# Half-position scans of a two-layer vision kernel: VectorE's weighing of a state moved behind the next state's scan

## What is computed

```python
def step(h, inp):
    dtt, ut, bt, ct = inp
    dA = jnp.exp(dtt[..., None] * A)
    h = h * dA + (dtt * ut)[..., None] * bt[:, :, None, :]
    y = jnp.einsum('bkdn,bkn->bkd', h, ct)
    return (h, y)
...
h = jax.nn.gelu(jnp.einsum('bsd,edh->ebsh', x, w1) + b1[:, None, None, :], approximate=False)
y = jnp.einsum('ebsh,ehd->ebsd', h, w2) + b2[:, None, None, :]
```

## Time and profile before

| what | us |
|---|---|
| median of 3 runs (lowest, highest) | 5605.96 (5604.6, 5613.72) |
| the profiled execution | 5607.85 |
| its span, first to last instruction | 5606.0 |
| a convolution stage, first scan to end of last (24 lanes) | 720.8 |
| a Mamba stage, the same (12 lanes) | 363.4 |
| all six stages together | about 3250 |

### The profile page before, as it was taken

How to read it: one execution, slowest core, us unless ns; L and a number is a source line. 1 busy time by engine, 2 the same in 40 slices (tenths; PEclk the granted TensorE clock), 3 DMA queues, 4 the chain that set the end, 5 groups by cost and what they waited for, 6 DMA issues and landing times. The chain is left out here.

```text
span 5606.0 us, 73119 instructions
## 1 busy us (share of the span) xinstructions
PE 4828.6 (86%) x23205; PEld 3411.3 (61%) x23205; DVE 4445.6 (79%) x4529; ACT 3634.0 (65%) x5725; POOL 3960.4 (71%) x3074
## 2 busy tenths in 40 slices
PE   7888797789898887888989888888998988888998
PEld 5776546656666645555666645565666654556777
DVE  6889838959999848977999957996999975896544
ACT  5666455448887757767878857775878865775222
POOL 5888619839999818857999935894999962984111
PEclk9999999989999998998999999998999999999999
DMA  5777607737877616647788724654877842562110
GB/s 206 263 252 264 211 10 258 252 132 254 287 268 268 226 34 219 224 135 250 260 280 271 269 69 171 220 183 161 281 266 276 271 166 102 201 216 93 43 43 29
DMA packets 356676, 1104.83 MB, mean 197 GB/s; under 512 B 33210, under 2 KB 121126, under 8 KB 354872
## 3 DMA queue, kind: packets, MB, share of 16 engines
q1 hardware_dynamic: 356280, 1100.06, 56.9%
HBM read 1086.24 MB, written 13.68 MB: 196 GB/s over the span
## 5 line engine op out<-in xcount | busy, mean ns | idle before, releaser
L1157 PE MATMUL banks<-ident,prod 128*128 128x128 f32 x4752 | 764.9, 287 | 392.5 <-DVE prod L1458 286.6
L1157 PEld LDWEIGHTS banks<-ident,prod 128*128 128x128 f32 x4752 | 556.8, 145 | 799.1 <-DVE prod L1458 557.8
L1449 DVE TENSOR_TENSOR_SCAN banks<-banks,h 128x512 f32<-128x512 f32 x594 | 723.3, 1218 | 85.8 <-ACT banks L1297 48.5
L1400 POOL TENSOR_TENSOR h<-lane,Bb 128x512 f32<-128x512 f32 x576 | 722.8, 1272 | 57.8 <-DMA Bb<-half_rows 33.8
L1297 ACT ACTIVATE banks<-lane,A 128x512 f32<-128x512 f32 x864 | 581.1, 686 | 251.6 <-DVE prod L1458 82.4
L1229 PE MATMUL banks<-w_a,Cb 128*128 128x384 f32 x1536 | 552.2, 488 | 0.0
L1449 DVE TENSOR_TENSOR_SCAN banks<-banks,half_carry_a,h 128x512 f32<-128x512 f32 x396 | 505.5, 1277 | 8.8 <-ACT banks L1297 4.9
L1400 POOL TENSOR_TENSOR h<-half_du_a,Bb 128x512 f32<-128x512 f32 x384 | 482.7, 1275 | 14.8 <-DMA Bb<-half_rows 10.1
L1297 ACT ACTIVATE banks<-half_delta_a,A 128x512 f32<-128x512 f32 x576 | 385.3, 685 | 151.5 <-DVE lane L1430 73.7
L1217 PE MATMUL banks<-big,w_a 128*128 128x256 f32 x1728 | 435.0, 394 | 1.0 <-DMA w_a<-w_in 0.8
L1458 DVE TENSOR_TENSOR prod<-banks,half_C_a 128x512 f32<-128x512 f32 x528 | 365.3, 692 | 73.4 <-DMA half_C_a<-half_rows 2.4
(11 more groups left out here) (471 smaller groups left out, 12291.6 us busy)
## 6 DMA issues: line engine op xcount, KB each, us to landing
Bb<-half_rows SPq DMA_DIRECT2D x576, 512.0 KB, 4.3
C_first<-rows SPq DMA_DIRECT2D x288, 512.0 KB, 5.4
Cb<-half_rows SPq DMA_DIRECT2D x288, 512.0 KB, 4.4
w_a<-w_in SPq DMA_DIRECT2D x256, 576.0 KB, 6.1
w_b<-w_in SPq DMA_DIRECT2D x128, 576.0 KB, 6.2
half_C_a<-half_rows SPq DMA_DIRECT2D x128, 512.0 KB, 6.7
Bb<-rows SPq DMA_DIRECT2D x96, 512.0 KB, 5.5
half_C_b<-half_rows SPq DMA_DIRECT2D x64, 512.0 KB, 6.6
```

Of the source, the lines that this page charges most:

```text
L1157: mm = eng.matmul(ps[:, 0, at], src[:, at], m.ident[:, :], start=n == 0 and k == 0, stop=added(s) == (i + 1) * N, is_transpose=True, skip_ ...
L1400: eng.tensor_tensor(m.dBu[:, s % DRIVES, :], m.du[i % 2], m.B[b % BRING][:, cols(s % 2)], ALU.mult).then_inc(st.dbu, 1)
L1449: eng.tensor_tensor_scan(flip(to), flip(slot(s)), flip(m.dBu[:, s % DRIVES, :]), initial, ALU.mult, ALU.add).then_inc(st.scanned, 1)
```

## The change

VectorE's `weigh(s - 1)` now stands behind `scan(s)`, no longer behind its own scan. TensorE's `add` of a state that VectorE weighs moves one step later as well, and with it the last `back`; `lane_order`, from which the counts of finished additions are taken, follows. Three products of TensorE go one step later too (`dt_product` from step 0 to 1, the gate products and the out products from step 6 to 7), since the banks that they take are freed by a `weigh` that is now later. What ScalarE, GpSimd and SyncE issue, and in which order, is the same as before.

```diff
--- before.py
+++ after.py
@@ -852,10 +852,10 @@
     COPY_AT, BACK_AT, TAKE_AT, SUM_AT, DELTA_AT = 3, 4, 7, 8, 4
     SKIP_TAKE_AT = 9
     BEHIND = 2
-    GATE_AT, PRODUCT_AT, OUT_AT, OUT_COPY_AT = 9, 6, 9, 11
+    GATE_AT, PRODUCT_AT, OUT_AT, OUT_COPY_AT = 9, 7, 9, 11
     gated = range(1, TILES + 1) if products is not None else ()
     product_of = {TILES + 2 + f: f for f in range(CT)} if products is not None else {}
-    INPUT_AT, INPUT_PLACE_AT, INPUT_TAKE_AT = 6, 9, 11
+    INPUT_AT, INPUT_PLACE_AT, INPUT_TAKE_AT = 7, 9, 11
     input_lanes = sorted(inputs.at) if inputs is not None else []
     input_of = {i: k for k, i in enumerate(input_lanes)}
     input_done = {inputs.at[i]: k + 1 for k, i in enumerate(input_lanes)} if inputs is not None else {}
@@ -883,7 +883,7 @@
 
         return s - pooled(s)
 
-    lane_order = [a for b in range(N) for a in ([] if by_pool(b) else [b]) +
+    lane_order = [a for b in range(N + 1) for a in ([b - 1] if b and not by_pool(b - 1) else []) +
                   ([b - BEHIND] if b >= BEHIND and by_pool(b - BEHIND) else [])]
 
     def added(s):
@@ -935,7 +935,7 @@
     downs = {pair_at(v, 2) + k: 2 * v + k for v in range(PAIRS_IN) for k in range(2)}
 
     evicts = {pair_at(v, 2) + 3: (v + 1) * 2 // PER - 1 for v in range(PAIRS_IN) if (v + 1) * 2 % PER == 0}
-    LAST = max([STEPS] + [s + 7 for s in evicts])
+    LAST = max([STEPS + 1] + [s + 7 for s in evicts])
 
     def chunk(k):
         return guests[k // E][0]
@@ -1235,9 +1235,9 @@
 
                 if s in ups and n == 0:
                     up(ups[s])
+                if s and s <= STEPS and not by_pool(s - 1):
+                    add(s - 1)
                 if s < STEPS:
-                    if not by_pool(s):
-                        add(s)
                     if n >= BEHIND and by_pool(s - BEHIND):
                         add(s - BEHIND)
                     if i and n == BACK_AT:
@@ -1248,11 +1248,11 @@
                         gate_product(input_of[i])
                     if fresh(i + 2) and n in (PROJECT_AT - 3, PROJECT_AT - 2):
                         project(i + 2, n - PROJECT_AT + 3)
-                    if i + 1 < LANES and n == DELTA_AT - 4:
+                    if i + 1 < LANES and n == DELTA_AT - 3:
                         dt_product(i + 1)
                     if i in turned_of and n == TURN_AT:
                         turn_residual(turned_of[i])
-                if s == STEPS - 1:
+                if s == STEPS:
                     back(LANES - 1)
                 if s in ups and n:
                     up(ups[s])
@@ -1489,15 +1489,16 @@
                 i, n = s // N, s % N
                 if s < STEPS:
                     scan(s)
-                    if not by_pool(s):
-                        weigh(s)
+                if s and s <= STEPS and not by_pool(s - 1):
+                    weigh(s - 1)
+                if s < STEPS:
                     if n == TAKE_AT and i:
                         take(i - 1)
                     if i in gated and n == GATE_AT:
                         gate(i - 1)
                     if i + 1 < LANES and n == DELTA_AT + 1:
                         delta(i + 1)
-                if s == STEPS - 1:
+                if s == STEPS:
                     take(LANES - 1)
                 if s in evicts:
                     evict(evicts[s])
```

## The result

The changed kernel takes 5653.8 us (median of 4 runs, 5644.7 to 5659.1) where the kernel before takes 5605.6 in the same job: a ratio of 1.0078, 95% interval 1.0061 to 1.0096. It is slower, by some 44 us. The forecast of 5616 was 38 us too low, and its likeliest band, 5594.8 to 5617.2 (0.43), was missed: slower had 0.38. The time lies inside the range, close to its upper end, and next to the rival on TensorE's clock (5659, chance 0.15).

The account below looks back on a forecast made before the run. VectorE was taken to bound the kernel; its 257 us saved would become stall on ScalarE's banks. 3 x 1.5 + 3 x 2.5, less about 2, gave + 10 on 5606: 5616 us, range 5570 to 5662.

Parts of the forecast that it names:

- the rival on TensorE's clock: TensorE idles some 3 us at every lane's turn, its clock falls, late up products delay a Gelu: 43 us, 5659; chance 0.15.
- What the change saves: VectorE's scan and weighing no longer wait for each other: 0.22 us off each of 1188 steps, 257 us of VectorE's time.
- The rival that the 0.13 us stay: VectorE's gap between scan and weighing stays even with a scan between, every link grows by 0.22: 5725; chance 0.03.
- The sentence quoted from the Trainium skill's page: "The semaphore costs nothing extra here": an operation flushes the pipeline anyway, so the 257 us would be nothing; the forecast disagreed.
- The ring takes it back: Banks are freed a scan later, ScalarE's lead shrinks from three scans to two, VectorE's saving is stall at states 3, 9, 14.
- the walk: Lane time followed link by link between scans 3, 6, 9, 14 and next 3; convolution averages 30.35 and 29.25 us; chance 0.62.
- The sum for the ring: Three convolution stages at + 1.5 and three Mamba stages at + 2.5, less about 2 for hidden stalls: + 10 us.
- the link that was to decide: The clock costs time once the second up product ends behind the first table load's start; 0.4 of 0.7 us margin left.
- a sign that the walk is wrong: Stalls released by GpSimd or TensorE instead of ScalarE's decays, or lanes of 28 us and less.
- The three products of TensorE that move are ready before their readers by more than a step: TensorE's products moved one step later were forecast to make no reader wait.
- GpSimd at nothing: GpSimd needs 27.6 us of a lane, 1 to 2 less than forecast lanes; cost nothing, up to 10 us if cover goes.
- The Mamba stages: Input lanes go from 31.44 to 32.5 us, other first-half lanes within 0.3, second-half lanes lose 0.2: + 2.5 a stage.

Follow-up runs that it names:

- run 4: Changed kernel with the experts' Gelu computed as Identity and the table loads left out (output not the reference's): 5502.7 us, ratio 0.9825.
- run 5: Kernel before with Gelu computed as Identity and the table loads left out (output not the reference's): 5557.8 us, ratio 0.9902.
- run 7: Run 6 plus the delta's product back at step 0 and state 0 weighed and added in its own step: 5596.8 us, ratio 0.9979.
- run 6: Changed kernel plus ten filler matmuls on TensorE at the lane's turn, in the convolution stages alone: 5613.5 us, ratio 1.0015.
- run 1: Changed kernel plus ten filler matmuls on TensorE at the lane's turn, in all stages: 5631.8 us, ratio 1.0046.
- run 2: Kernel before plus six filler matmuls on TensorE in its idle time at the lane's turn: 5602.0 us, ratio 0.9995.
- run 11: Changed kernel without fillers, state 0 weighed and added in its own step, delta's product back at step 0: 5643.5 us, ratio 1.0080.
- run 3: Changed kernel with VectorE weighing states 5, 9 and 14 in their own step, TensorE's order unchanged: 5632.7 us, ratio 1.0052.
- run 8: Run 7 with states 0, 5, 9 and 14 weighed and added in their own step in all stages: 5594.8 us, ratio 0.9970.
- run 10: Run 7 with early states 0, 5, 9, 14 (convolution) and 0, 6 (Mamba), plus four drive buffers instead of three: 5563.0 us, ratio 0.9919.

## Why the prediction was right or wrong

- **What the change saves: right.** 0.21 us between a dependent and an independent pair were forecast from the rows, and the pairs came out so. The rival that the 0.13 us stay is refuted. The sentence quoted from the Trainium skill's page "VectorE: DVE Perf Modes", section "The DRAIN you can't avoid", is said there of a chain of eight copies, and does not hold for this pair. The rows differ by 0.21 us (scan ends to weighing, + 0.13 behind its own scan and - 0.08 at 1428.44 above).
- **The ring takes it back: right, and shown.** Each piece of the walk is within 0.07 us of its undisturbed lanes, and with the blocks cut the change gains 43 us on the old order by the ratios (runs 4 and 5).
- **The sum for the ring: 22 us too high.** With both other costs mended (run 7) the kernel is 0.21% faster than before, 12 us, where the walk gave + 10 (run 7 also weighs state 0 early, which was not walked). The lanes are not what is off: behind the first three of the first stage they take 30.39 and 29.06 us in run 7, and 30.46 and 29.26 in run 6, where the walk has 30.35 and 29.25. Part of it is the base. The forecast took 29.75 us for a first-half lane before the change; the mean over the lanes after the first three is 29.97 (5.64, 6.62, 8.32, 9.39) and 29.76 for the second instead of 29.7, so each convolution stage was forecast 3.3 us too dear: it was to get 1.5 us longer and takes 718.4 us in run 7 against 721.3. Another 3.7 us a stage lie behind the last scan, a stretch that wasn't walked (157.4 us before, 153.7 in run 7).
- **TensorE's clock: the cost that was given as a rival, 0.15.** Its size was nearly right (43 us forecast, some 35 measured), but by luck: it was 0.4 us for a waiting Gelu in each of 108 lanes, and what came is some 13 us in each of the three convolution stages, for other readers. The measured time lies in the range because this size had been taken in. Right was how it starts: the copy of the sum is later, the idle time doubles, the clock falls. What was wrong is the link that was to decide. I made it whether the second up product ends behind the start of the first table load. It does: it ends at 1733.47 + 1.94 = 1735.41, and the load starts at 1734.32, 1.1 us earlier, where the forecast left a margin of 0.4. But the load waits for nothing, the Gelu behind it starts at 1735.62, and the whole convolution stage has one wait of 1.7 us there. ScalarE's timeline in that lane:

```profile
1733.61 0.69 ACT L1297 ACTIVATE banks<-lane,A 128x512 f32<-128x512 f32 x1 [1.09 <-DVE prod L1458]
1734.32 1.28 ACT L1341 ACT_TABLE_LOAD   x1
1735.62 0.84 ACT L1341 ACTIVATE Cb<-banks,vec 128x256 f32<-128x256 f32 x2
```

  Who waits is VectorE, for the turned sum and the down products that stand behind the ups in TensorE's queue. Its waits of the first convolution stage (us, times, longest):

```profile
DVE xt_a L1485 <- PE banks L1229: 13.0, 9, 1.6
DVE big L2946 <- PE banks L1201: 4.8, 4, 2.1
```

  The pieces show the same. With the fillers (run 6) those from 6 to 9, where the turned sum is taken and the eviction stands, add up to 10.3 us less in the first stage (176.2 to 165.9), and those from 3 to 6, where ScalarE waits for the delta's product, to 5.2 less (139.6 to 134.4). Stalls released by TensorE were named as a sign that the walk is wrong; here they came beside it.

  I had followed the first reader of the late product and not the queue behind it. With that reader alone the chance of 0.15 looked fair; with the queue it should have been the likeliest case, as the lane of the earlier trace rows already showed the low level before the change. Runs 1 and 6 agree with the warning of gaps in the Trainium skill's page "TensorE: Matmul & The Clock Gate", section "Why this matters for your kernels", though the gaps here (1.16 and 2.48 us) are shorter than the one that it names. Run 2 adds a limit: what low clock the kernel before has costs it nothing.
- **"The three products of TensorE that move are ready before their readers by more than a step": wrong for one of them.** The delta's activations waited for theirs in 9 of the first stage's lanes, up to 1.0 us each, and behind them the piece from 3 to 6 grew to 6.1 to 6.5. Run 7 puts 17 to 20 us on it, together with the early weighing of state 0, once the clock is mended; run 11 finds nothing to 10 us while it is not.
- **GpSimd at nothing: right for this change,** with 11.2 us of wait in the stage against 9.7. It was the next in line as soon as the ring was loosened (runs 3, 8 and 10).
- **The Mamba stages: + 7.5 forecast, + 14.6 measured over the three, and + 4.1 in run 7.** From state 6 on the input lanes came as walked. Part of the surplus is the delta's product: 3 to 6 is up to 0.8 us longer in lanes 1, 2 and 4 of the first stage than the 5.49 us of run 7. The larger part is lane 3, which was to stay within 0.3 us: it takes 32.50, 34.15 and 34.16 us in the three stages, where it took 30.07. VectorE stands there for the last down product ahead of an eviction, which it didn't wait for before:

```profile
2230.66 1.14 DVE L1485 SCALAR_TENSOR_TENSOR late_xt<-banks,weights,late_xt 128x384 f32<-128x384 f32 x2 [3.18 <-PE banks L1229]
```

  The waits are 3.18, 4.82 and 4.45 us. With fillers in these stages too (run 1) they are 2.07 each, so some of it is the clock and some the later turn itself. But the same fillers make lane 9 take 33.12 us instead of 29.14 in the first stage, and the stages get no shorter.

So 44 us measured are, mended in the order of runs 6 and 7, some 35 of clock in the convolution stages and some 20 of a late product (with the early weighing of state 0), less 12 by which run 7 is faster than the kernel before. Mended the other way round (run 11, then run 7), the clock's share is 41 us by the profiled stages and 57 by the ratios.

## What to carry to other kernels

When work is moved a step later, follow two chains: the buffer that comes free later, up to the long block of the engine that refills it, and the queue of each engine that is made to wait, down to the last reader of what stands in it. A ring of buffers makes every such delay a question of which element counts: here four of the sixteen states in the convolution stages and two in the Mamba stages are freed early, and the others give the saving. And TensorE, whose granted clock fell behind its idle times here, can be slower for less work, so a longer idle time at one fixed place of a loop is priced with all that its queue does after it.

## What the runs showed of the hardware

- Ten idle-time matmuls at the lane's turn took the low-clock time of a convolution stage from 109 to 10 us, and TensorE's busy time from 668 to only 679, for 460 instructions more (x3180 to x3640). At 2.50 us a lane the fillers are 57 us, so the work that must be done got 46 us cheaper.
- After an idle time of 2.48 us the first additions still took 0.63 us, then the delta product 1.81 and an up product 2.93 (1.12 and 1.56 behind the fillers), and the next up product 1.94. Behind 1.16 us of idle time before the change TensorE was slow too, at a granted clock of 0.50, for a shorter stretch. What idle time is short enough was not tried.
- A table load costs 1.28 us of ScalarE each, and two of them with their Gelus hold a four-bank ring 4.2 us. Taking them out was worth 142 us in the order with a lead of two scans and 55 in the one with three (by the ratios). The price of a block depends on the lead, not on its length alone.
